# First layer norm of a graph network: x in column halves by two queues, scaled by ScalarE, lower parts computed between the halves of the next statistics

## What is computed

```
xn = layernorm(x)                      # (x - mean) / sqrt(var + 1e-5), per row
x  = x + gnn0(xn, edges, types) + mix0(xn)
x  = x + ffn0(layernorm(x))
xn = layernorm(x)
x  = x + gnn1(xn, edges) + mix1(xn)
x  = x + ffn1(layernorm(x))
```

## Time and profile before

| | before |
|---|---|
| median of 3 runs | 1891.42 us (1891.12 to 1891.88) |
| profiled execution, its own time | 1892.73 us |
| its span | 1891.2 us |
| busy: PE | 1805.9 us (95%) |
| busy: DVE | 1030.4 us (54%) |
| busy: ACT | 478.5 us (25%) |
| busy: POOL | 701.6 us (37%) |
| mean granted TensorE clock | 0.974 |

### The profile page before, as it was taken

How to read it: one execution, slowest core, us unless ns; L and a number is a source line. 1 busy time by engine, 2 the same in 40 slices (tenths; PEclk the granted TensorE clock), 3 DMA queues, 4 the chain that set the end, 5 groups by cost and what they waited for, 6 DMA issues and landing times.

```text
span 1891.2 us, 28873 instructions
## 1 busy us (share of the span) xinstructions
PE 1805.9 (95%) x10036; PEld 1488.1 (79%) x10036; DVE 1030.4 (54%) x2570; ACT 478.5 (25%) x1055; POOL 701.6 (37%) x609
## 2 busy tenths in 40 slices
PE   6999999999999999999999999864999999999999
PEld 4876689987777778777777887752899888878987
DVE  7888999997254452525454256777632225262311
ACT  3139956662011110101011045342100000111100
POOL 2110000003534436363443543200385562345862
PEclk9999999999999999999999999955999999999999
DMA  4532222213312122231313533110254351113322
GB/s 133 154 110 74 78 86 80 73 62 127 95 38 83 46 70 68 65 90 37 88 44 120 171 96 97 45 46 6 81 169 141 115 152 54 35 56 111 95 73 66
DMA packets 129282, 162.23 MB, mean 86 GB/s; under 512 B 14288, under 2 KB 75368, under 8 KB 128922
## 3 DMA queue, kind: packets, MB, share of 16 engines
q1 hardware_dynamic: 100848, 120.93, 21.4%
q10 hardware_dynamic: 22250, 23.53, 3.9%
q0 software_dynamic: 6080, 16.40, 2.9%
HBM read 135.51 MB, written 25.30 MB: 85 GB/s over the span
## 4 chain that ended last, share of the span: by engine, by line
PE 83%; DVE 7%; ACT 5%; issue 2%; DVEq 1%; DMA 1%; POOL 0%; SPq 0%; ACTq 0%
PE ps L367 21%; PE ps L368 21%; PE ps L369 21%; PE ps L1236 9%; PE ps L892 3%; ACT sc_col L838 2%; ACT sc_row L837 1%; PE ps L1201 1%; DVE w_lo L318 1%; PE ps L881 1%; PE ps L1156 1%; DMA nat<-in_x 1%; ACT w_hi L313 1%; PE ps L1183 1%; PE ps L1718 1%
## 5 line engine op out<-in xcount | busy, mean ns | idle before, releaser
L367 PE MATMUL ps<-w_hi,xt_hi 128*125 128x512 f32 x1320 | 539.4, 409 | 8.4 <-DVE xt_lo L549 3.5
L256 POOL TENSOR_TENSOR w_hi<-w_stage,zero 128x512 fp32r<-128x512 f32 x256 | 276.3, 1079 | 696.3 <-PE ps L369 684.9
L368 PE MATMUL ps<-w_lo,xt_hi 128*125 128x512 f32 x1320 | 523.1, 396 | 0.0
L369 PE MATMUL ps<-w_hi,xt_lo 128*125 128x512 f32 x1320 | 521.6, 395 | 0.0
L259 POOL TENSOR_TENSOR w_lo<-w_stage,w_hi 128x512 fp32r<-128x512 f32 x256 | 347.3, 1357 | 20.1
L367 PEld LDWEIGHTS ps<-w_hi,xt_hi 128*125 128x125 f32 x1320 | 246.8, 187 | 66.2 <-DVE xt_lo L549 4.4
L369 PEld LDWEIGHTS ps<-w_hi,xt_lo 128*125 128x125 f32 x1320 | 246.2, 187 | 63.4
L368 PEld LDWEIGHTS ps<-w_lo,xt_hi 128*125 128x125 f32 x1320 | 246.6, 187 | 53.5
L367 PE MATMUL ps<-xt_hi,w_hi 128*128 128x314 f32 x736 | 250.4, 340 | 1.4 <-DVE ring L2420 0.7
L369 PE MATMUL ps<-xt_hi,w_lo 128*128 128x314 f32 x736 | 225.9, 307 | 0.0
L368 PE MATMUL ps<-xt_lo,w_hi 128*128 128x314 f32 x736 | 225.7, 307 | 0.0
(11 more groups left out here) (390 smaller groups left out, 2417.1 us busy)
## 6 DMA issues: line engine op xcount, KB each, us to landing
w_stage<-in_stream SPq DMA_DIRECT2D x374, 256.0 KB, 2.7
pre<-ring POOLq DMA_DIRECT2D x30, 250.0 KB, 3.9
a_qt<-pre_t SPq DMA_DIRECT2D x18, 312.5 KB, 3.9
a_qt<-pre_t ACTq DMA_DIRECT2D x14, 312.5 KB
pre_t<-ring_t POOLq DMA_DIRECT2D x12, 312.5 KB, 2.8
pre_t<-ring_t ACTq DMA_DIRECT2D x12, 312.5 KB
a_vx<-pre SPq DMA_DIRECT2D x9, 312.5 KB
nat<-pre SPq DMA_DIRECT2D x2, 1250.0 KB
```

The costliest lines, as they stand in the source:

```text
L256: POOL.tensor_tensor(w_hi[:, q, :], w_stage[:, q % NST, :], zero[:].to_broadcast([128, 512]), ALU.add).then_inc(S("hi_done"), 1)
L367: PE.matmul(dst, l_hi, r_hi, start=first, stop=False)
L368: PE.matmul(dst, l_hi, r_lo, start=False, stop=False)
L369: return PE.matmul(dst, l_lo, r_hi, start=False, stop=last)
```

## The change

Four edits, all in the first norm:

1. Tiles 0, 1 and 2 of x are loaded in halves of 512 columns, the left half on SP's queue and the right half on ACT's. Tile 3 follows on ACT's queue instead of POOL's; tile 4 stays with POOL. Tiles 0 and 1 have a semaphore for each half, so that the statistics of the left half can start alone.
2. The scaling moves from DVE to ACT: DVE computes minus mean times scale (one value per row, `first_scale`), and ACT scales the tile in two halves. PE's transposes, ACT's copies and DVE's subtractions each wait by halves.
3. On DVE, the lower parts of tile m-1 now stand between the two halves of the statistics of tile m (for m of 2 and more).
4. ACT's list is written anew, with the chunks' high parts at other places. The transposes keep their places in PE's list.

Other semaphores were merged to free some; their waits differ in the number only (those lines are left out).

```diff
+    def load_half(eng, m, j):
+
+        c = slice(j * 512, (j + 1) * 512)
+        eng.dma_start(nat[:, m, c], a["x"][m * P:(m + 1) * P, c]).then_inc(S(f"ld_x{m}_{j}" if m < 2 else "ld_x2"), 16)
+
...
     for m in range(3):
-        load_x(SP, m)
+        load_half(SP, m, 0)
+        load_half(ALE, m, 1)
+    load_x(ALE, 3)
     for c in range(NST):
         load_chunk(c, c)
...
-    POOL.wait_ge(S("ld_x2"), 16)
-    for m in (3, 4):
-        load_x(POOL, m)
+    POOL.wait_ge(S("ld_x2"), 32)
+    load_x(POOL, 4)
...
-    def first_norm(m):
+    def first_scale(m):
 
         DVE.wait_ge(S("x_dev"), m + 1)
         newton_row(m)
-        ln_tile(nat, nat, m).then_inc(S("x_norm"), 1)
+        DVE.scalar_tensor_tensor(m_first[:, m:m + 1], mv[:, m, 0:1], -1.0, rs[:, m:m + 1], ALU.mult, ALU.mult)
+        DVE.drain().then_inc(S("h_scale"), 1)
+
+    def first_norm(m):
+
+        ALE.wait_ge(S("h_scale"), m + 1)
+        for j in range(2):
+            c = slice(j * 512, (j + 1) * 512)
+            ALE.activation(nat[:, m, c], nat[:, m, c], ACT.Identity, scale=rs[:, m:m + 1],
+                           bias=m_first[:, m:m + 1]).then_inc(S("x_norm" if j else "x_norm_a"), 1)
...
     def first_turn(m):
 
-        PE.wait_ge(S("x_norm"), m + 1)
         if m >= 2:
             PE.wait_ge(S("x_low"), m - 1)
         for k in range(KT):
+            if k % 4 == 0:
+                PE.wait_ge(S("x_norm" if k else "x_norm_a"), m + 1)
...
-    first_stats(0)
-    first_norm(0)
-    first_stats(1)
-    first_norm(1)
-    first_low(0)
-    first_stats(2)
-    first_low(1)
-    first_norm(2)
...
+    for m in range(T):
+        first_stats(m, 0)
+        if m >= 2:
+            first_low(m - 1)
+        first_stats(m, 1)
+        first_var(m)
+        first_scale(m)
+        if m == 1:
+            first_low(0)
+    first_low(T - 1)
...
     first_dev(0)
+    first_norm(0)
     first_dev(1)
     first_high(0)
+    first_norm(1)
     split_act(0)
     first_high(1)
+    first_dev(2)
     split_act(1)
-    first_dev(2)
-    for c in (2, 3):
-        split_act(c)
+    first_norm(2)
+    split_act(2)
+    first_high(2)
     first_dev(3)
-    first_high(2)
-    for c in (4, 5, 6):
-        split_act(c)
+    split_act(3)
+    split_act(4)
+    first_norm(3)
+    split_act(5)
+    first_high(3)
     first_dev(4)
-    first_high(3)
+    split_act(6)
+    first_norm(4)
     split_act(7)
     first_high(4)
...
     for rows in ((0, 1), (2, 3, 4)):
-        if rows[0]:
-            PE.wait_ge(S("x_low"), T)
         for k in range(KT):
+            if k % 4 == 0:
+                PE.wait_ge(S("x_low" if k else "x_low_a"), rows[-1] + 1)
```

More of the change, by code:

```diff
@@ L515, in first_view, with first_stats, first_var @@
         return ps[:, first_banks(m)[j], 0:4 * P].rearrange("p (k n) -> p k n", k=4)
-    def first_stats(m):
-        DVE.wait_ge(S(f"ld_x{m}"), 16)
-        stats_tile(nat, m)
+    def first_stats(m, j):
+        if m < 2:
+            DVE.wait_ge(S(f"ld_x{m}_{j}"), 16)
+        elif j == 0:
+            DVE.wait_ge(S(f"ld_x{m}"), 32 if m == 2 else 16)
+        stats_tile(nat, m, (j,))
+    def first_var(m):
         DVE.drain()
@@ L558, in first_high @@
     def first_high(m):
-        ALE.wait_ge(S("x_turn"), m + 1)
         for j in range(2):
-            t_ = ALE.activation(xt_hi[:, 4 * j:4 * j + 4, m * P:(m + 1) * P], first_view(m, j), ACT.Copy)
-        t_.then_inc(S("x_hi"), 1)
+            ALE.wait_ge(S("x_turn" if j else "x_turn_a"), m + 1)
+            ALE.activation(xt_hi[:, 4 * j:4 * j + 4, m * P:(m + 1) * P], first_view(m, j),
+                           ACT.Copy).then_inc(S("x_hi" if j else "x_hi_a"), 1)
     def first_turn(m):
-        PE.wait_ge(S("x_norm"), m + 1)
         if m >= 2:
@@ L1649, in norm_rows @@
             c = slice(0, 512)
-            DVE.scalar_tensor_tensor(o[:, c], o[:, c], r, lnb[:, c], ALU.mult, ALU.add).then_inc(S("h_half"), 1)
+            DVE.scalar_tensor_tensor(o[:, c], o[:, c], r, lnb[:, c], ALU.mult, ALU.add).then_inc(S("h_scale"), 1)
             c = slice(512, D)
@@ L1727, in sum_dve @@
             DVE.wait_ge(S("rk_part"), i + 1)
-            DVE.tensor_copy(q_part7[:, 0:columns], ps[:, 0, 0:columns]).then_inc(S("rk_copied"), 1)
+            DVE.tensor_copy(q_part7[:, 0:columns], ps[:, 0, 0:columns]).then_inc(S("rk_some"), 1)
             beside()
@@ L1789, in find_rank @@
             DVE.wait_ge(S("rk_part"), ROUNDS + 1)
-            DVE.tensor_copy(q_part7[:, 0:1], ps[:, 0, 0:1]).then_inc(S("rk_copied"), 1)
+            DVE.tensor_copy(q_part7[:, 0:1], ps[:, 0, 0:1]).then_inc(S("rk_some"), 1)
         DVE.tensor_copy(q_top[:], q_took[:])
@@ L2089, in tile_low @@
         for j in range(2):
-            DVE.wait_ge(S("x_hi"), o + m + 1) if j else DVE.wait_ge(S("x_hi_a"), o - AGAIN + m + 1)
+            DVE.wait_ge(S("x_hi"), o + m + 1) if j else DVE.wait_ge(S("x_hi_a"), o + m + 1)
             DVE.tensor_tensor(xt_lo[:, 4 * j:4 * j + 4, m * P:(m + 1) * P], tile_view(m, j, o),
@@ L2097, in tile_turn @@
         if o == AGAIN:
-            PE.wait_ge(S("x_norm_a"), m + 1)
+            PE.wait_ge(S("x_norm_a"), AGAIN + m + 1)
         else:
@@ L2233, in again_norm @@
     def again_norm(m):
[L2235 removed]
+        ALE.wait_ge(S("h_scale"), AGAIN + 1 + m + 1)
         norm_act(m).then_inc(S("x_norm"), 1)
@@ L2343, in build @@
     for m in range(T):
-        PE.wait_ge(S("x_low_a"), m + 1)
+        PE.wait_ge(S("x_low_a"), AGAIN + m + 1)
         PE.wait_ge(S("down_free"), 6 if m < 2 else 2 * T)
```

28 lines of the change are left out of this document (10 added, 18 removed).

## The result

| | before | with the change |
|---|---|---|
| median | 1891.61 us (1891.12 to 1891.88, 5 runs) | 1900.01 us (1898.49 to 1901.13, 5 runs) |
| ratio to before, 95% interval | | 1.0045 [1.0034, 1.0055] |
| profiled execution, its own time | 1892.73 us | 1898.49 us |
| its span | 1891.2 us | 1897.0 us |
| busy PE, DVE, ACT, POOL | 1805.9, 1030.4, 478.5, 701.6 us | 1805.4, 1026.8, 486.1, 701.4 us |

What follows compares the result with a forecast made beforehand. PE, busy 95% of the span, was taken to bound the kernel, so only its idle stretches count. Terms +0.5, +4.7 and +1.4 gave +6.6 us on the median 1891.42: 1898.0 us, range 1894.2 to 1901.2.

Steps and rivals of the forecast that it cites:

- G: Mark: PE's first matmul of row tiles 2 to 4, at 38.57 us before the change; forecast between 43.8 and 45.2.
- A: Shift of T2 by the changed start, with the first product 1.15 us earlier: +0.5 us, from -0.3 to +2.6.
- B: Stretch from T2 to G: 17.2 us instead of 12.5 through waits before chunks 3 and 6, +4.7 us (3.7 to 5.7).
- C: Clock loss from PE idling in the waits before chunks 3 and 6: +1.4 us, bounds 0 and 3.4.
- T2: Mark: PE's first transpose of tile 2, at 26.08 us before the change; forecast at 26.55.
- I take 18.0: Start of ACT's high part of chunk 0, whose landing was put between 17.1 and 20 us: 18.0 us assumed.
- T3: Mark: tile 3's transposes on PE, forecast 7.3 us after T2, when chunk 3 ends.
- the ring: Transposes, copies, lower part, next tile's statistics, root, chunk's high part, POOL's part: 5.9 us from T2 to chunk 3, again to chunk 6.
- The double rate of x: Rival: second queue's halves use other DMA engines, PE starts 4.8 us early; +3.0 us, 1894.4 us, chance 0.11.
- Chunk 0 late: Rival: chunk 0 lands at 20 because tile 3 moves beside it; +8.7 us, 1900.1 us, chance 0.14.
- Cheap waits: Rival: clock stays up, the ring takes 5 us instead of 5.9, nothing lands later; +3.4 us, 1894.8 us, chance 0.05.
- faster: Rival: shorter way from x to PE gains 4.8 us, later waits of 1.2 us vanish; 1885.4 us, chance 0.04.

## Why the prediction was right in place and sign, and where its sizes failed

**Forecast against measurement.** +6.6 us were forecast; G's shift is +7.0, the medians' 8.4, and 1900.0 lies inside the range, 2.0 above the forecast. Of the signs named in advance, these came: waits for POOL's low parts ahead of chunks 1, 3 and 6, the high part of chunk 3 right behind a root, a first product near 20 (19.26, by 0.7 too early), 0.76 for each half of the norm, a stretch at half clock (behind the second longest wait, not the longest). G came at 45.55, just outside the 43.8 to 45.2 that was named. The sum at G is off by only 0.4 us because two errors offset each other, 1.0 too high in A and 1.35 too low in B and C; that much of it is luck.

**Term A was 1.0 us too high** (+0.5 forecast, -0.5 measured at T2), in two places. The first product came at 19.26 instead of 19.95, 1.84 us early instead of 1.15. What sets it, in the forecast and in the trace, is chunk 0, and the step that failed is "I take 18.0": the chunk's high part starts at 17.18, and with 0.63 and POOL's part it is ready at 19.16. The step "I take 0.4", by which tile 1 comes later, failed too, but cost nothing here. Both halves' statistics end at 13.0 instead of 13.8, so the right half was there by about 12.3, no later than the 12.3 to 12.75 of whole tiles by one queue; and a start of the statistics 1.1 us later (old loads) leaves the first product at 19.55. The second place is chunk 1: "PE waits 1.4 us" was 0.72, because its low part is ready 3.6 us after the first product instead of 4.0, and chunk 0 keeps PE for 2.9 us of these instead of 2.6. The two chunks together took 5.6 us instead of 5.2.

**Terms B and C were 1.35 us too low together** (6.1 forecast, 7.46 measured). By pieces, from the rows above:

```
                      forecast   measured
T2 to chunk 3            5.9       6.25
chunk 3 to T3            1.4       2.23
T3 to chunk 6            5.9       6.14
chunk 6 to G             4.0       5.33
sum                     17.2      19.95
T2 to G before          12.5      12.49
term C                  +1.4      (in the pieces)
```

- T2 to chunk 3: the ring is right to 0.35 us. Its first step was undersized: ACT's copy begins 1.07 after T2 instead of 0.55, because tile 2's transposes still run at the slow pace (1.61 us for 8 instead of 1.02); with tile 3 by POOL they run at the fast one, and the copy begins 0.63 after T2. The rest took less than added up.
- Chunk 3 to T3: forecast without a wait; PE waits 0.58 for the norm. The step that failed is that DVE "loses 5 scalings of 0.81 and gains 5 small steps" with "nothing of it reaches PE". The new small step (L555) and Newton's last one ahead of it (L548) stretched to 1.17 and 1.07 us beside POOL. I had this only as the upper bound of B ("if POOL's work stretches DVE's small steps again"); here it comes once in full (tile 3) and once for L548 alone (1.08 at tile 4), since the ring starts POOL's part and these steps at nearly the same moment.
- Chunk 6 to G: at half clock chunk 6 takes 2.53 us (40.22 to 42.75) where chunk 7 takes 1.47, and tile 4's transposes 1.33 where tile 3's took 1.02: some 1.4 us, the size of term C, at another place than forecast. Chunk 7's wait of 0.45 did not come.

**Rivals.** The double rate of x is refuted: 0.33 of the engines and 128 GB/s with two queues. By the rules that the prediction quoted from the Trainium skill (DMA: Bandwidth & Descriptors), the engines for a tile of 125 rows are 5 and a second queue brings no bandwidth; the trace now agrees with both. Chunk 0 late is refuted (17.18). Cheap waits and faster fell with the ring.

**The cause, where the prediction was vague.** It wrote the ring as one chain through both engines' lists and stressed the chunks behind the roots. The runs separate the two: DVE's order alone makes +8.0 us on the kernel before and gives back 5.5 on the changed one; ACT's order gives back about 2, hardly clear of the scatter, and nothing once DVE's is mended. What is left then is 3.4 us over before. Tile 3 back on POOL's queue takes away 2.4 of them. Chunk 7's earlier place on top of that takes 0.6, within the scatter, and tile 3's root ahead of tile 2's copies 1.6, which leads 1.7 us below before. The early start (first product between 19.05 and 19.86 with ACT's scaling, 20.67 to 21.10 without) reaches G in full only in the kernel that mends all of these.

**What stays open.** Why chunk 7's earlier place did not show in the median, and what lowers the clock behind one wait and not behind another.

## What to carry to other kernels

On an engine that runs its list in order, a step put between two halves of another inherits, for everything behind it, the wait of what it depends on. Here it tied tile m's norm to tile m-1's transposes, and cost 8 us. Before moving a step forward, follow it once around: which engine feeds it, what that engine's list has in front, and whether the engine that must not idle has as much work as the ring is long (PE had 3.0 us of work against a ring of 6.25 here). And where several hand-written lists change at once, run each list's old order alone: the part that looked guilty gave back at most a quarter, the other two thirds.

## What the runs showed of the hardware that was not expected

**DVE's small steps behind POOL.** A product of two columns of 125 values takes DVE 0.16 us when POOL is idle, and 0.66 to 1.08 us beside it. Rows of the changed kernel's timeline, around chunk 1's part on POOL:

```profile
21.56 1.26 POOL L282 TENSOR_TENSOR w_lo<-w_stage,w_hi 128x512 fp32r<-128x512 f32 x1 [2.40 <-ACT w_hi L319]
21.94 0.15 DVE L546 TENSOR_SCALAR t<-t 125x1 f32<-125x1 f32 x1 [0.49 <-issue]
22.18 0.66 DVE L548 TENSOR_TENSOR rs<-rs,t 125x1 f32<-125x1 f32 x1
22.92 0.16 DVE L555 SCALAR_TENSOR_TENSOR m_first<-mv,rs 125x1 f32<-125x1 f32 x1
```

L546 has one tensor as input and is as short as ever (0.15), though DVE idles 0.49 us ahead of it for a reason that the profile does not name; L548 has two and ends at 22.84, with POOL's instruction (22.82); L555, with two, takes 0.16 once POOL is done. At 30.74 and 31.89 each of L548 and L555 ends with one of POOL's two. The Trainium skill (GPSIMD Engine Reference, Specifications) says that GpSimd's memory interfaces are shared with VectorE, with contention for VectorE instructions that have two inputs in SBUF or run in a two-port mode; the trace agrees for the first kind, and the doubled scaling L345 (1.68 against 0.81), which has one tensor input, could be the second, but no run here shows its mode. So a step's size says little about its price beside POOL: at 30.74 and 31.89 two such steps in a row took as long as POOL's two instructions.

**Which wait costs the clock.** In one execution 3.25 us of waiting left the granted clock at 1.00, and behind 1.96 us it was at 0.50; in another of the same kernel it was at 0.50 behind both 2.58 and 2.02, the second time only 1.5 us after the wait. With ACT's order undone 2.29 us left it at 1.00, and it was at 0.50 behind 1.22. Waits of 1.76 us (DVE's order undone) and 1.52 (both undone) left it at 1.00. The length of a wait alone does not tell.

**A slow pace that the clock column does not show.** After the first product the matmuls of 512 columns start 0.43 us apart, later 0.23, while the column of the granted clock reads 1.00 in both stretches. The trace's own list of granted clocks has its first entry, full speed, at 25.70 us before the change and at 26.80 with it, which is where the pace doubles. So the 1.00 ahead of these moments is not a reading, and the 0.43 has to be taken from the rows.

**Halves on two queues.** The two halves of tile 0 land 0.9 us apart (7.29 and 8.21), not together, and the second no earlier than the whole tile did by one queue (7.92 to 8.26 in three traces). Only the statistics of the first half gain from it.
